# Wider spacing of the layer-norm steps behind the output projection, and score maxima that end one slot earlier

## The reference

```python
x = L0_attn_h                                    # (8, 1024, 512)
x = x + layernorm(attention(layernorm(x), Wqvk, Wo))
x = x + layernorm(ffn(layernorm(x), W1, b1, ..., W2, b2))

def attention(h, Wqvk, Wo):
    q, v, k = split((h @ Wqvk))                  # 16 heads x 32
    scores = causal(q @ k.T) / sqrt(512)
    wv = softmax(scores) @ v
    return wv @ Wo
```

## Time and profile before

| | us |
|---|---|
| median of 3 runs | 3627.89 |
| lowest, highest | 3616.19, 3633.15 |
| the profiled execution | 3645.58 |
| its span | 3643.8 |
| attention in it | about 630 to 2190 |

### The profile page before, as it was taken

One profiled execution on the slowest core, in us unless ns is written; L12 is line 12 of the kernel. 1 busy time (PEld: TensorE's weight loads), 2 busy tenths in 40 slices (PEclk: granted clock), 3 DMA queues, 4 the chain that ended last, 5 costly groups with the idle time before them and its releaser, 6 DMA issues. The chain is left out here.

```text
span 3643.8 us, 69980 instructions
## 1 busy us (share of the span) xinstructions
PE 3210.2 (88%) x25389; PEld 1800.5 (49%) x25389; DVE 2468.9 (68%) x4477; ACT 2125.5 (58%) x2708; POOL 1468.3 (40%) x1087
## 2 busy tenths in 40 slices
PE   6999996888888887888888773999999999999998
PEld 2444442655555565656555541444444444444443
DVE  5444445988878787878788846566666666666665
ACT  2222221977878797969787873445454455445544
POOL 0000001988888898989898880000000000000000
PEclk9999996988898989999999986999999999999999
DMA  3334433122221312222222213001100000000000
GB/s 128 124 120 139 133 108 95 48 60 73 60 74 44 95 49 79 65 64 67 66 66 72 67 36 124 1 24 35 36 24 24 24 24 24 24 24 24 24 24 24
DMA packets 183089, 219.95 MB, mean 60 GB/s; under 512 B 15184, under 2 KB 129936, under 8 KB 182288
## 3 DMA queue, kind: packets, MB, share of 16 engines
q1 hardware_dynamic: 182800, 215.83, 19.0%
HBM read 130.84 MB, written 84.41 MB: 59 GB/s over the span
## 5 line engine op out<-in xcount | busy, mean ns | idle before, releaser
L929 POOL TENSOR_TENSOR a_prob_lo<-a_prob,a_prob_hi 128x1024 f16<-128x1024 f32 (+1 forms) x640 | 1237.7, 1958 | 203.4 <-ACT a_prob_hi L821 202.5
L849 DVE TENSOR_REDUCE a_mx<-a_pw 128x1 f32<-128x512 f32 (+3 forms) x1216 | 755.2, 657 | 142.0 <-PE a_pw L707 102.1
L814 ACT ACTIVATE a_prob<-a_pst,a_lift,a_exp_scale 128x1024 f32<-128x1024 f32 (+1 forms) x640 | 717.0, 1120 | 192.3 <-PE a_pst L756 97.8
L1376 PE MATMUL f_py<-f_w,f_act 128*128 128x512 f16 x3072 | 707.2, 380 | 22.1 <-DVE f_work L1142 12.8
L1366 PE MATMUL f_ph<-f_xT,f_w 128*128 128x512 f16 x3072 | 706.0, 380 | 0.4 <-issue 0.4
L821 ACT ACTIVATE a_prob_hi<-a_prob 128x1024 f16<-128x1024 f32 (+1 forms) x640 | 622.4, 973 | 0.0
L702 PE MATMUL a_pw<-a_kp,a_qp 96*128 96x512 f16 (+3 forms) x1536 | 499.5, 362 | 138.1 <-DVE a_mx L849 101.3
L1097 POOL TENSOR_TENSOR f_ve<-f_mv,f_eps 128x4 f32<-128x4 f32 x32 | 9.0, 282 | 1384.9 <-DVE f_mv L1123 1384.9
L751 PE MATMUL a_pst<-a_qp,a_kp 98*128 98x256 f16 (+1 forms) x2560 | 497.3, 279 | 78.6 <-ACT a_prob L814 55.8
L1314 ACT ACTIVATE f_hidden_work<-f_ph,f_turn,f_fold 128x512 f32<-128x512 f32 x256 | 199.0, 777 | 597.2 <-PE f_ph L1366 596.0
L1376 PEld LDWEIGHTS f_py<-f_w,f_act 128*128 128x128 f16 x3072 | 298.6, 98 | 379.8 <-issue 21.8
(11 more groups left out here) (174 smaller groups left out, 3934.7 us busy)
## 6 DMA issues: line engine op xcount, KB each, us to landing
qk_parts<-q_stage SPq DMA_DIRECT2D x128, 256.0 KB, 2.1
a_qp<-qk_parts SPq DMA_DIRECT2D x192, 128.0 KB, 2.6
a_kp<-qk_parts SPq DMA_DIRECT2D x192, 128.0 KB, 2.8
v_parts<-q_vstage SPq DMA_DIRECT2D x16, 1056.0 KB, 5.1
a_vt<-v_parts SPq DMA_DIRECT2D x32, 528.0 KB, 4.1
q_x<-in_L_attn_h_dram SPq DMA_DIRECT2D x16, 1024.0 KB, 7.7
a_xr<-in_L_attn_h_dram SPq DMA_DIRECT2D x64, 256.0 KB, 3.2
x<-a_y SPq DMA_DIRECT2D x64, 256.0 KB, 2.1
```

What stands on the lines that cost most here:

```text
L814: act.activation(prob[:, k % PR, :, off:QC], pst[:, k % 2, :, off:QC], ACT.Exp, scale=exp_scale[:, :], bias=lift[:, :]).then_inc(exp_done, 1)
L849: dve.tensor_reduce(out, src, AX_X, ALU.max).then_inc(released, 1)
L929: pool.tensor_tensor(prob_lo[:, k % HR, :, off:QC], prob[:, k % PR, :, off:QC], prob_hi[:, k % HR, :, off:QC], ALU.subtract).then_inc(lo_d ...
L1376: last = pe.matmul(py[:, t, :], act_r[:, f % AR, b, t * P:(t + 1) * P], w2s[:, a, f, :], start=(f == 0 and j == 0), stop=(f == NF - 1 and ...
```

## The change

Two tables of numbers change. The steps behind a wo item at slot s move from s+1, s+2, s+3, s+4 to s+2, s+4, s+6, s+7. The pieces are spread anew: slots 3 and 12 hold three instead of two, and slot 16 none instead of two; the max item stays at slot 17. `TAIL`, the number of slots after the last batch, follows from `WO_STORE` and grows from 15 to 18.

```diff
-PIECES_AT = dict(enumerate((3, 3, 3, 2, 2, 2, 1, 2, 2, 3, 2, 2, 2, 2, 2, 3, 2)))
+PIECES_AT = dict(enumerate((3, 3, 3, 3, 2, 2, 1, 2, 2, 3, 2, 2, 3, 2, 2, 3)))
...
-WO_SMALL, WO_NORM, WO_ADD, WO_STORE = 1, 2, 3, 4
+WO_SMALL, WO_NORM, WO_ADD, WO_STORE = 2, 4, 6, 7
```

## The result

| | before | after |
|---|---|---|
| median of 4 runs, us | 3625.39 | 3667.84 |
| lowest, highest | 3616.19, 3633.15 | 3658.29, 3673.30 |
| ratio after / before, 95% interval | | 1.0115, 1.0080 to 1.0151 |
| span of the profiled execution | 3643.8 | 3671.0 |

What follows compares the result with a forecast made beforehand. POOL was taken to bound the attention, closely followed by ACT. Terms of 7.9 us a batch times 7.5 gave 59 us off 3645.6, then 17.7 less for the median: 3569 us, range 3510 to 3625.

Steps and rivals of the forecast that it cites:

- What bounds the kernel, and the norm gaps: Attention: POOL is the bound; each normalisation empties its queue to one slot, leaving gaps of 0.89 and 1.85 us.
- The spacing's terms: Gains of POOL idle time per batch: unit 0 3.0, start of unit 1 1.4, unit 3 3.2 and 1.0 us.
- PE takes over: Rival, chance 0.14: DVE's waits and low clocks grow with denser work, leaving 2.8 us a batch; 3617 us.
- SP, the charge of 2.0 us a batch: Slot 17, units 3 and 0: tile's store ahead of the maxima's delays PE; charged 2.0 us, bounds 0 and 8.
- The chain: Unit's end: tile store, x load, maxima DMAs landing T+3.8, PE's scores, ACT, then POOL's slot 19 low part at T+6.9.
- T: The time at which POOL's add of slot 16 ends, for which the tile's store waits.
- The pieces, credited with 1.3 us a batch: Slot 16 emptied of pieces, so PE's wait at the max item goes; 1.3 us a batch, bounds 0 to 1.8.
- moves work, not its amount: The piece added at slot 12 was said only to shift work, with no gain or loss counted.
- The 0 us for the piece that reads q and k early: Slot 3's added piece reads their late half one slot sooner: 0 to 1 us of PE, hidden under POOL's queue.
- The rule against it: DVE/GpSimd port lock: 128 divisions each approach 2.3 us, 140 us more of DVE's time; sum kept as DVE had slack.
- The stores of the maxima decide: Rival, chance 0.11: POOL runs dry 4 to 6 us at each of 14 boundaries, eating the spacing's gain; 3647 us.
- The signs that were to show the forecast wrong: Maxima DMA wait over 8 us, POOL idle over 3 us at slots 0-3 of units 1, or unit 0 at 55, PE full.

Runs made afterwards that it cites:

- run 4: Wider spacing with the old pieces, and SP storing the maxima ahead of the tile in slot 17, against the unchanged kernel: 3612.8 us, ratio 0.9959.
- run 12: Whole change, maxima stored first, division with one input in PSUM, join over one tile, all computed, against the unchanged kernel: 3517.1 us, ratio 0.9685.
- run 11: Unchanged kernel but reciprocals in a PSUM bank, so the division reads one SBUF tile, and join over one tile; all computed: 3547.1 us, ratio 0.9770.
- run 10: Whole change, maxima stored first, join over one input, division replaced by a same-size copy, against the unchanged kernel: 3514.2 us, ratio 0.9678.
- run 8: New pieces with old spacing, join over one input, division replaced by a same-size copy, against the unchanged kernel: 3551.7 us, ratio 0.9788.
- run 1: Wider spacing alone, pieces as before, against the unchanged kernel: 3655.5 us against 3631.5, ratio 1.0101.
- run 9: Whole change with its store order, join over one input, division replaced by a same-size copy, against the unchanged kernel: 3554.8 us, ratio 0.9788.
- run 3: Whole change, but SP stores the maxima ahead of the tile in slot 17, against the unchanged kernel: 3648.4 us, ratio 1.0051.
- run 5: Unchanged kernel with one piece moved from slot 16 to slot 3, old spacing: 3659.6 us, ratio 1.0085.
- run 6: Unchanged kernel with one piece moved from slot 16 to slot 12, old spacing: 3650.3 us, ratio 1.0036.
- run 2: New pieces alone, steps behind a tile spaced as before, against the unchanged kernel: 3669.1 us, ratio 1.0119.

## Why the prediction was wrong

- **What bounds the kernel, and the norm gaps: right in mechanism, too large in size.** POOL's idle time sets the pace, and ACT's wait at L826 fell from 143.8 to 21.9 us (under 50 was said). The spacing's terms, 3.0 + 1.4 + 3.2 + 1.0 a batch, make 65 us. It measured 19 us (run 4) beside the divisions and 30 to 37 without their stands (run 12 against 11, 10 against 8). From run 8 to 10 POOL's idle time fell by 2.4 us in unit 0, 1.4 at the start of unit 1 and 0.9 in unit 3: the 1.4 came in full, but behind the wo items of slots 2 and 14 new gaps opened. "PE takes over" had that mechanism, as a rival.
- **SP, the charge of 2.0 us a batch: mis-sized.** The chain was right to some tenths of a microsecond up to PE's scores (T+4.1 against T+3.8). But it charged 15 us in all, and the order costs 41 to 43 us where it is isolated (runs 1 and 4, 9 and 10) and 20 with the new pieces (after and run 3): 3 to 6 us a batch, inside its bounds of 0 to 8, but not at the value taken. What failed is what comes after the scores: PE stood 3.4 us, not 6, and still came back at half clock for 6.8 us, so that ACT had the first scores 2.35 us after PE began them, not 1.3. POOL got slot 19's part at T+8.3 instead of T+6.9 and ran dry again at slot 2. And the loss was put at the end of unit 0, as the 3.54 us of the loop's turn would cover the other boundary; they did not: with the maxima first POOL's idle time at slot 19 falls by 3.0 us at the end of unit 3 and by 1.9 at the end of unit 0 (run 9 to run 10, averages of the loop's six batches).
- **The pieces, credited with 1.3 us a batch, "moves work, not its amount": this step failed outright.** Alone they cost 38 us, next to the late store of the whole change nothing that can be told. The wait at the max item was to be near zero and was 37.3 us, since L852 stood longer in the freed slot; before and after, its row (ns: shortest, middle, longest) reads

```profile
L852 DVE TENSOR_TENSOR a_mx<-a_mx x32: 175/1460/2109, 620.6 to 2108.5; 128x16 f32<-128x16 f32 x32
```
```profile
L852 DVE TENSOR_TENSOR a_mx<-a_mx x32: 174/2041/2190, 621.8 to 2139.8; 128x16 f32<-128x16 f32 x32
```

  for 16 elements of each partition. The 0 us for the piece that reads q and k early held: only in runs 10 and 12 does PE wait for that load, 1.1 to 2.2 us once in each of seven batches, and in the loop POOL idles nowhere in that unit.
- **The rule against it was set aside for a wrong reason.** It was priced as more time of DVE and dismissed because DVE had 3 us left in a unit. The total of the divisions did not grow with the change: 128 of 1.25 us on average in both traces (159.8 and 159.5 us together). What hurts is not DVE's sum but where a stand of 2 us falls: ahead of a piece for which PE waits, with PE's clock at half behind it (0.53 in the first of the two rows of the result). The rule of the Trainium skill, "SBUF — State Buffer", section "Who interferes with whom", that a DVE instruction with two SBUF inputs waits out POOL's, is borne out: with one of the inputs in PSUM each took 0.42 us (run 11). Where it speaks of one instruction, the trace shows a wait through up to four of them (below).
- **The rivals.** "The stores of the maxima decide" had 0.11 and gave 3647, where 3667.8 was measured; its sign came true, with losses by the pieces as much as by the stores. The signs that were to show the forecast wrong did not come: the wait for the DMA stayed under 4.7 us, where over 8 was named, and POOL idled 0.9 us on average at slots 0 to 3 of unit 1, where over 3 was named, and unit 0, at 61 us, had PE busy for 50 of them, not full. The loss lay at places for which no sign was named: slot 19 and slots 12 to 15. Without the store order alone the change is still 0.5% slower (run 3), without the new pieces alone 1.0% (run 1).

Open: which division of which slot turns against PE when a piece moves. Runs 5 and 6 show that both single moves raise the mean division (from 1.25 to 1.47 and 1.31 us) but not a rule by which to place a piece. One pattern is on record: all divisions of over 2.5 us, eight of 7.3 to 8.9 us in the traces of the changed kernel and of runs 1, 2, 3 and 5, are that of block 3 of unit 1, which DVE reaches in slot 5 of unit 2; before and runs 4 and 6 have none. One or two of them make only a part of the loss. Nor does a run tell how much of each loss comes by the stand of PE itself and how much by the half clock behind it.

## What to carry to other kernels

When an instruction's duration varies fivefold for the same shape, treat the slow ones as a wait: find what it shares, and price the wait by who stands behind it, not by the engine's total. A step that is put later in an engine's list must be followed on the DMA queue as well, where it may now stand ahead of something urgent. And take such a stand away before tuning the order around it: the same table of pieces cost 38 us with the stands and 1.4 us without them.

## What the runs showed of the hardware

A division of DVE can stand through several instructions of POOL, not only the one in flight. In the last batch of the changed kernel one took 7.68 us, and POOL ran four low parts (7.38 us) from the same moment:

```profile
2110.38 7.68 DVE L876 TENSOR_TENSOR a_o<-a_osum,a_rden 128x256 f32<-128x256 f32 x1
```
```profile
2110.39 7.38 POOL L929 TENSOR_TENSOR a_prob_lo<-a_prob,a_prob_hi 128x1024 f16<-128x1024 f32 x4
2124.28 4.39 POOL L929 TENSOR_TENSOR a_prob_lo<-a_prob,a_prob_hi 128x1024 f16<-128x1024 f32 x2 [6.51 <-ACT a_prob_hi L821]
```

PE stood 7.29 us at a piece for DVE, ACT 6.91 us for PE's scores, and POOL itself then idled 6.51 us, for the work that DVE had held back. With one input of the division in PSUM and the join over one tile (run 11), the mean granted clock of the attention was 0.96 instead of 0.91 and the kernel took 2.3% less time, though DVE is the busiest engine in none of the stretches of the earlier trace rows. And the stands of PE of 2.91 us at the third piece of slot 12 and of 3.44 us at the unit's end were followed by 3.4 and 6.8 us at half clock.
